# Attention and quantized feed-forward on one core: work moved at both ends of the attention loop

## The chip, the cores and the metric

The kernel runs on one core of one Trainium2 chip. The metric is device microseconds of one launch, lower is better. Times of before are from three runs, and from one profiled execution whose trace is quoted below.

## The reference

The input x is 16 batches of 512 rows of 256 numbers. Per batch, with LN a normalization over the last axis without weights:

```python
x = x + attention(LN(x))
x = x + ffn(LN(x))
# attention: 16 heads of 16 columns; xh is LN(x) cut into heads
xw  = einsum('bhtd,hde->bhte', xh, w_att_val)
att = softmax(einsum('bhte,bhse->bhts', xw, xh) / sqrt(16))
o   = einsum('bhts,bhsd->bhtd', att, (LN(x) @ wv_w.T + wv_b) in heads) @ out_w.T + out_b
# ffn: every operand of every product first goes through fp4_quant_dequant (blocks of 16)
gate, up = fp4_linear(y, w_gate), fp4_linear(y, w_up)      # 704 columns
ffn      = fp4_linear(silu(gate) * up, w_down)
```

fp4_quant_dequant divides each block of 16 by its scale (largest magnitude / 6), rounds to the FP4 grid and multiplies back.

## The kernel before

Three blocks of engine programs follow each other, with a barrier of all engines between them. Rows stay in SBUF in x_all, 64 tiles of 128 rows (four per batch), for the whole kernel. "Tile n" of the feed-forward part is row n of x_all.

**first_block** loads batches 0 and 1, normalizes batch 0, turns it, and casts it into a high and a low part (xh and xl, likewise qh and ql, together the tile splits) for exact products in a fast format. SyncE stores these to DRAM (x_rows, q_rows; semaphores stored0 and stored1, one per half of the heads) and reads them back as stacks: x_stack and q_stack of a quad (four heads) hold 64 rows per head pair, so that one product gives scores exact to float32. load_stacks (L146) issues six DMAs per quad; stack_loaded of a quad counts them. VectorE's low_q (L337) makes ql, statistics (L312) starts the normalization of batch 1, and v_dense, the values, comes last (L364).

**attention_block** works in quads, 64 of them, each in four steps j. For quad i+2 TensorE makes score products of queries by keys into a ring of PSUM banks (max_scores, L769) and VectorE reduces each to row maxima (reduce_max, L1058); GpSimd splits the maxima in two (split_maxima, L595), VectorE turns them, and ScalarE's queue stores them to DRAM and loads them back as max_stack (store_maxima, L988, load_maxima, L994). For quad i TensorE makes the scores of keys by queries and adds the maxima by a second product (key_scores, L782), ScalarE takes exponentials (L924), TensorE weighs the values (weigh_values, L793). In the gaps (IN_STEP) stand the preparation of batch b+1 ("x0", "q0", "x1", "q1", "v0", "v1") and the end of batch b-1: "rows" (turn the weighed values), "turn0" and "turn1" (turn the normalized outputs), "proj0" and "proj1" (output projection, then the residual add on VectorE, L1127). The order of each engine is written out by hand; semaphores alone connect them. SyncE stores and loads stacks of batch b+1 during batch b (L745). ScalarE's queue opens the block with copy_weights (L1012), twelve DRAM to DRAM DMAs into slabs, which batch b quantizes three at a time. After the loop, the rest of batch 15 is finished on its own (rows3, turn0, turn1, proj0, proj1).

Before the first batch stands a prologue of sixteen max_scores calls (two products each), quads 0 and 1; the first step's scores follow it:

```python
for g in range(2):
    for n in range(PAIRS * TT):
        max_scores(-1, g + 2, n)
pe.wait_ge(pool_set, POOL_SET)
batch(0)
```

**ffn_block** works in rounds n, each engine with its own body(n, u). In round n TensorE does turn_h(n-1), gate_up(n+1), turn_x(n+2), down(n-1) (L1433); VectorE normalizes tile n+4, quantizes tile n+3, multiplies gate by up for tile n and quantizes that (L1301). x's absolute values and the gates are ScalarE's, the scaling back GpSimd's. Rounds begin at -5: `ROUNDS = (-5, (1, TILES // 4 - 2), TILES + 2, 4)`, so rounds -5 to 0 fill the pipeline.

## Time and profile before

| What | us |
|---|---|
| median of 3 runs (1507.13 to 1508.17) | 1507.44 |
| profiled execution | 1504.88 |
| its span | 1502.9 |
| busy: TensorE | 1427.5 (95%) |
| busy: VectorE | 1267.9 (84%) |
| busy: ScalarE | 865.6 (58%) |
| busy: GpSimd | 658.7 (44%) |

PE is TensorE's products and PEld its weight loads, DVE is VectorE, ACT is ScalarE, POOL is GpSimd; ACTq and SPq are the DMA issues of ScalarE and SyncE. A timeline row gives start, duration, engine, line, what is written from what, the count, and in brackets how long the engine was idle before and what released it. An x16 of fp32 products is eight calls. The granted clock of TensorE is a share of 2.4 GHz, so 0.50 is 1.2 GHz.

### The profile page before, as it was taken

Reading aid. Unit: us, or ns where it says so; the run is one execution under the profiler, and the core shown is the slowest. Engines: PE = TensorE matmul, PEld = TensorE weight load, DVE = VectorE, ACT = ScalarE, POOL = GpSimd, SP = SyncE. Lnnn points to the kernel's source line nnn. Section 1 sums busy time; section 2 is a strip of 40 time slices with the busy share of each in tenths; the row PEclk is TensorE's granted clock in tenths of the full one; section 3 lists DMA queues with packets and bytes.
Section 4 is the critical chain, followed back from the end, with each engine's and each line's share of the span. In section 5 each row is a group of like instructions: output and inputs, shape, how many; then the busy total and the mean of one; then the engine's idle time right before and its main releaser. Section 6 shows DMA issues by size and latency. Waiting matters only on the chain. (4 is left out here: it accounts for less than half of the span.)

```text
span 1502.9 us, 32223 instructions
## 1 busy us (share of the span) xinstructions
PE 1427.5 (95%) x8562; PEld 886.5 (59%) x8562; DVE 1267.9 (84%) x2644; ACT 865.6 (58%) x1730; POOL 658.7 (44%) x910
## 2 busy tenths in 40 slices
PE   3799999999999999999999998699999999999998
PEld 2355555555555555555555554467777777777776
DVE  4888888888888888888888883499999999999995
ACT  1477777777777767777777767333333333333332
POOL 2346546546546546545545421143434434343341
PEclk7799999999999999999999999899999999999999
DMA  8655555555555556556555460000000000000000
GB/s 235 174 150 163 144 142 167 139 140 169 138 140 173 136 138 175 134 138 176 133 138 168 119 170 16 0 12 18 14 17 14 17 14 17 17 14 17 14 18 22
DMA packets 99433, 148.09 MB, mean 99 GB/s; under 512 B 20928, under 2 KB 58176, under 8 KB 99392
## 3 DMA queue, kind: packets, MB, share of 16 engines
q1 hardware_dynamic: 76832, 135.38, 33.0%
q10 hardware_dynamic: 22560, 12.21, 3.2%
q8 instruction: 21, 0.34, 0.1%
q14 instruction: 20, 0.16, 0.0%
HBM read 85.02 MB, written 65.27 MB: 100 GB/s over the span
## 5 line engine op out<-in xcount | busy, mean ns | idle before, releaser
L1064 DVE TENSOR_REDUCE neg_max<-ring 128x1 f32<-128x512 f32 x1024 | 642.8, 682 | 109.8 <-PE ring L779 106.2
L924 ACT ACTIVATE probs<-scores 128x512 f32<-128x512 f32 x1024 | 531.4, 603 | 189.7 <-PE scores L790 178.0
L1410 PE MATMUL gu_bank<-splits,f_x_T 128*128 128x352 f32 x1024 | 315.4, 462 | 0.9 <-ACT f_x_T L1388 0.9
L779 PE MATMUL ring<-x_stack,q_stack 64*128 64x512 f32 x1024 | 234.3, 456 | 33.5 <-DVE neg_max L1064 18.7
L806 PE MATMUL ring<-probs,v_quad 128*32 128x512 f32 x2048 | 247.3, 601 | 4.2 <-DVE neg_max L1064 4.1
L1410 PEld LDWEIGHTS gu_bank<-splits,f_x_T 128*128 128x128 f32 x1024 | 190.7, 191 | 96.8 <-ACT f_x_T L1388 1.6
L779 PEld LDWEIGHTS ring<-x_stack,q_stack 64*128 64x128 f32 x1024 | 98.5, 188 | 189.4 <-DVE neg_max L1064 138.0
L787 PE MATMUL scores<-q_stack,x_stack 64*128 64x512 f32 x1024 | 206.8, 399 | 2.6 <-ACT probs L924 2.6
L790 PE MATMUL scores<-max_stack,max_ones 64*128 64x512 f32 x1024 | 203.3, 392 | 0.0
L1243 POOL TENSOR_TENSOR f_rstd<-f_mean_var,eps 128x1 f32<-128x1 f32 x64 | 43.2, 676 | 294.5 <-DVE f_mean_var L1354 294.5
L623 POOL TENSOR_TENSOR pv_rows<-pv_more,pv_rows 128x512 f32<-128x512 f32 x64 | 82.0, 1282 | 198.9 <-ACT pv_more L930 198.9
L1373 ACT ACTIVATE h_T<-h_bank 128x512 f32<-128x512 f32 (+1 forms) x128 | 55.8, 488 | 173.1 <-PE h_bank L1420 173.1
L1428 PE MATMUL y_bank<-splits,h_T 128*128 128x256 f32 x640 | 148.9, 380 | 1.1 <-ACT h_T L1373 1.1
L806 PEld LDWEIGHTS ring<-probs,v_quad 128*32 128x32 f32 x2048 | 54.0, 109 | 126.4 <-issue 77.3
L1428 PEld LDWEIGHTS y_bank<-splits,h_T 128*128 128x128 f32 x640 | 116.9, 191 | 14.8 <-DVE x_all L1344 0.8
L787 PEld LDWEIGHTS scores<-q_stack,x_stack 64*128 64x128 f32 x1024 | 97.6, 186 | 24.0 <-ACT probs L924 12.6
L790 PEld LDWEIGHTS scores<-max_stack,max_ones 64*128 64x128 f32 x1024 | 97.4, 186 | 20.7
L1253 POOL TENSOR_TENSOR hq<-h_level,h_scale 128x704 f32<-128x704 f32 x64 | 88.7, 1385 | 30.0 <-DVE h_level L1299 30.0
L600 POOL TENSOR_TENSOR max_cols<-neg_max,one 128x16 fp32r<-128x16 f32 x64 | 13.8, 216 | 183.6 <-DVE neg_max L1064 183.6
L1388 ACT ACTIVATE f_x_T<-x_bank 128x256 f32<-128x256 f32 x64 | 24.6, 384 | 119.5 <-PE x_bank L1398 119.4
L1294 DVE SCALAR_TENSOR_TENSOR h_level<-h_mag,h_units 128x704 f32<-128x704 f32 x64 | 57.1, 892 | 41.5 <-ACT h_mag L1366 41.5
L1380 ACT ACTIVATE gate<-gu_bank 128x352 f32<-128x352 f32 x128 | 58.7, 458 | 41.1 <-PE gu_bank L1410 41.1
(115 smaller groups left out, 1983.6 us busy)
## 6 DMA issues: line engine op xcount, KB each, us to landing
x_rows<-splits SPq DMA_DIRECT2D x128, 256.0 KB, 3.0
x_stack<-x_rows SPq DMA_DIRECT2D x128, 256.0 KB, 4.3
q_stack<-q_rows SPq DMA_DIRECT2D x256, 128.0 KB, 4.3
q_rows<-splits SPq DMA_DIRECT2D x64, 256.0 KB, 2.2
out_dram<-x_all SPq DMA_DIRECT2D x64, 128.0 KB, 1.7
x_all<-in_L_attn_x_dram ACTq DMA_DIRECT2D x14, 512.0 KB, 4.1
w_raw<-slabs SPq DMA_DIRECT2D x14, 192.0 KB, 4.4
slabs_kept<-w_turned SPq DMA_DIRECT2D x14, 192.0 KB, 4.3
```

The source lines that it names most:

```text
L623: pool.tensor_tensor(pv_rows[g % 2][:, :], pv_more[:, :], pv_rows[g % 2][:, :], ALU.add)\
L779: pe.matmul(bank(tiles[m])[:, :], row_tile(q_stack[q], m)[:, p, s * P:(s + 1) * P], row_tile(x_stack[q], m)[:, p, :], start=True, stop=Tru ...
L787: pe.matmul(scores[ROWS * p + m][:, :], row_tile(x_stack[g], m)[:, p, j * P:(j + 1) * P], row_tile(q_stack[g], m)[:, p, :], start=True, st ...
L790: pe.matmul(scores[ROWS * p + m][:, :], row_tile(max_ones, m)[:, 0, :], row_tile(max_stack[g % 2], m)[:, p, :], start=False, stop=True).th ...
L806: m = pe.matmul(bank(tile)[VW * h:VW * h + VW, :], v[q][:, j, h, :], probs[j][:, k, :], start=(j == steps[0]), stop=(j == steps[1]))
L924: act.activation(probs[j][:, k, :], scores[k][:, :], ACT.Exp).then_inc(p_ready, 1)
L1064: dve.tensor_reduce(neg_max[g % 2][:, at:at + 1], tile[:, :], AX.X, ALU.max, negate=True).then_inc(m_used, 1)
L1253: pool.tensor_tensor(blocks(out), blocks(level), spread(scale, BLK), ALU.mult).then_inc(done, 1)
L1294: dve.scalar_tensor_tensor(out=level, in0=mag, scalar=SHIFT_MIN, in1=units, op0=ALU.max, op1=ALU.subtract).then_inc(step, 1)
L1380: act.activation(gate[1 - u][:, k, :], gu_bank[k][:, :], ACT.Silu).then_inc(gate_done, 1)
L1410: m = pe.matmul(gu_bank[c][:, :], x_T[u][:, a, :], gate_up_T[:, a, c * CH:(c + 1) * CH], start=(a == 0), stop=(a == HALVES - 1))
L1428: m = pe.matmul(y_bank[:, :], h_T[u][:, k, :], down_T[k][:, :], start=(k == 0), stop=(k == len(SLICES) - 1))
```

## The change

The change has four parts. *Stores and loads of batch 0:* before the first barrier only the first half of the heads is stored and only quad 0 is loaded, x_stack by SyncE and q_stack by ScalarE; quad 1, the second half's stores and quads 2 and 3 follow the barrier. VectorE's low_q(0) comes before statistics(1). *First scores:* the scores of quad 0's first step stand inside the prologue, before the sixth max_scores call of quad 1 (AHEAD = 5). *Weight copy:* the twelve DMAs move from ScalarE's queue to SyncE's, behind all stack loads of batch 0 and a wait for quad 0's maxima. *Seam:* the class FirstX holds the steps on x of the feed-forward part, on tiles of attention that are free by then (v_dense, raw_x, raw_q); tiles 0 and 1 are quantized and tile 2 normalized in quads 2 and 3 of batch 15, and the rounds begin at -1 (TensorE and ScalarE: -2). The end of batch 15 moves into these rounds. The turned maxima of quad 1 are also taken two reductions sooner.

```diff
@@ first_block, SyncE, ScalarE, VectorE
-            for a in range(HALVES):
-                sp.wait_ge(xl_done, a + 1)
-                store(a, x_rows, (xh, xl, xl, xh))
-            for a in range(HALVES):
-                sp.wait_ge(ql_done, a + 1)
-                store(a, q_rows, (qh, ql))
-
+            sp.wait_ge(xl_done, 1)
+            store_parts(sp, 0, 0, x_rows, (xh, xl, xl, xh), stored)
+            sp.wait_ge(ql_done, 1)
+            store_parts(sp, 0, 0, q_rows, (qh, ql), stored)
             sp.wait_ge(bias_loaded, 32)
-            for g in range(2):
-                load_stacks(sp, 0, g, x_stack, q_stack, x_rows, q_rows, stored, stack_loaded)
+            sp.wait_ge(stored[0], STORES)
+            load_x_stack(sp, 0, 0, x_stack, x_rows, stack_loaded)
...
             move(1)
+            act.wait_ge(stored[0], STORES)
+            load_q_stack(act, 0, 0, q_stack, q_rows, stack_loaded)
...
             low_x(1)
+            low_q(0)
             dve.wait_ge(x_second, 16)
             statistics(1)
-            low_q(0)
             low_q(1)
@@ attention_block, one batch early on VectorE, ScalarE, GpSimd
+    EARLY_DVE = {(2, 0): (("statistics", 0), ("statistics", 1)), (2, 1): (("normal", 0), ("statistics", 2)),
+                 (2, 2): (("units", 0), ("normal", 1), ("statistics", 3)),
+                 (3, 0): (("levels", 0), ("units", 1), ("normal", 2)), (3, 2): (("levels", 1),)}
+    EARLY_ACT = {(2, 3): 0, (3, 1): 1}
+    EARLY_POOL = {(2, 1): (("deviation", 0), ("deviation", 1)), (2, 2): (("deviation", 2),), (2, 3): (("deviation", 3),),
+                  (3, 1): (("back", 0),), (3, 3): (("back", 1),)}
@@ attention_block, SyncE
+            load_x_stack(sp, 0, 1, x_stack, x_rows, stack_loaded)
+            store_parts(sp, 0, 1, x_rows, (xh, xl, xl, xh), stored)
+            store_parts(sp, 0, 1, q_rows, (qh, ql), stored)
             for g in range(2, QUADS):
                 load_stacks(sp, 0, g, x_stack, q_stack, x_rows, q_rows, stored, stack_loaded)
+            sp.wait_ge(max_loaded[0], 16 * ROWS)
+            copy_weights()
             sp.wait_ge(w_copied, 16 * COPIES)
             load_weights(0)
             batch(0)
@@ attention_block, TensorE
             for g in range(2):
                 for n in range(PAIRS * TT):
+                    if (g, n) == (1, AHEAD):
+                        pe.wait_ge(pool_set, POOL_SET)
+                        step_scores(0, 0, 0, True)
                     max_scores(-1, g + 2, n)
-            pe.wait_ge(pool_set, POOL_SET)
...
             weigh_values(B, 0, True)
-            for kind in [kind for kind in ALL if kind in FINISH]:
-                other(kind, B)
@@ attention_block, ScalarE
-            copy_weights()
+            load_q_stack(act, 0, 1, q_stack, q_rows, stack_loaded)
             store_maxima(0, 0)
             load_maxima(0, 0)
...
             end_half(LAST, QUADS - 1)
-            turn("turn0", B)
-            turn("turn1", B)
@@ ffn_block
-    ROUNDS = (-5, (1, TILES // 4 - 2), TILES + 2, 4)
+    EARLY = -1
+    ROUNDS = ((1, TILES // 4 - 2), TILES + 2, 4)
...
+            pool.tensor_tensor(pv_rows[1][:, :], pv_more[:, :], pv_rows[1][:, :], ALU.add).then_inc(end_summed, 1)
...
+                if isinstance(n, int) and n == -1:
+                    weigh_last()
+                if isinstance(n, int) and n == 0:
+                    add_last()
...
+                if isinstance(n, int) and n in (-2, 0):
+                    a = (n + 2) // 2
+                    act.wait_ge(end_turned, a + 1)
+                    act.activation(o_T[a][:, :], turn_bank[a], ACT.Copy).then_inc(end_moved, 1)
...
+                if isinstance(n, int) and n == -2:
+                    turn_last(0)
+                if isinstance(n, int) and n == -1:
+                    rows_last()
+                if isinstance(n, int) and n == 0:
+                    pe.wait_ge(end_weighed, 1)
+                    turn_last(1)
+                    pe.wait_ge(end_moved, 2)
+                    project_last(0)
+                    project_last(1)
+                    pe.wait_ge(end_added, 2)
+                    pe.wait_ge(padded, 1)
```

What moves can be seen on two engines at three places. The lines are those of each kernel's own file. First SyncE's queue in the first block, before (x_rows and q_rows are stores, the stacks loads; the pair of stack rows comes four times):

```order
L209 DMA x_rows<-splits 128x512 x8
L209 DMA q_rows<-splits 128x512 x4
L152 DMA x_stack<-x_rows 64x1024
L156 DMA q_stack<-q_rows 32x1024 x2
L152 DMA x_stack<-x_rows 64x1024
L156 DMA q_stack<-q_rows 32x1024 x2
```

and in the change, where the L228 branch is the barrier:

```order
L184 DMA x_rows<-splits 128x512 x4
L184 DMA q_rows<-splits 128x512 x2
L162 DMA x_stack<-x_rows 64x1024 x2
L228 UNCONDITIONAL_BRANCH
L735 UNCONDITIONAL_BRANCH
L162 DMA x_stack<-x_rows 64x1024 x2
L184 DMA x_rows<-splits 128x512 x4
L184 DMA q_rows<-splits 128x512 x2
L162 DMA x_stack<-x_rows 64x1024 x2
L172 DMA q_stack<-q_rows 32x1024 x4
```

Two quads' loads stood ahead of the barrier, and now only quad 0's x part does; the second half's stores follow it.

Second, TensorE from the first barrier on, before (products into the ring are max_scores, the others key_scores):

```order
L767 UNCONDITIONAL_BRANCH
L779 MATMUL ring<-x_stack,q_stack 128x512 x34
L787 MATMUL scores<-q_stack,x_stack 128x512 x2
L790 MATMUL scores<-max_stack,max_ones 128x512 x2
L787 MATMUL scores<-q_stack,x_stack 128x512 x2
L790 MATMUL scores<-max_stack,max_ones 128x512 x2
L779 MATMUL ring<-x_stack,q_stack 128x512 x4
```

and in the change:

```order
L830 UNCONDITIONAL_BRANCH
L842 MATMUL ring<-x_stack,q_stack 128x512 x26
L850 MATMUL scores<-q_stack,x_stack 128x512 x2
L853 MATMUL scores<-max_stack,max_ones 128x512 x2
L850 MATMUL scores<-q_stack,x_stack 128x512 x2
L853 MATMUL scores<-max_stack,max_ones 128x512 x2
L842 MATMUL ring<-x_stack,q_stack 128x512 x12
L850 MATMUL scores<-q_stack,x_stack 128x512 x2
```

The first step's eight score products move from behind all 32 products of the prologue (two of the 34 are batch 0's) to behind the 26th.

Third, TensorE from the last products of attention (L838, L846, L853 are rows3, the turns and the projections; L1410 gate and up, L1420 the transposes of h), before:

```order
L838 MATMUL ring<-ident,pv_rows 128x128 x4
L806 MATMUL ring<-probs,v_quad 32x512 x8
L838 MATMUL ring<-ident,pv_rows 128x128 x4
L846 MATMUL ring<-ident,o_rows 128x128 x8
L853 MATMUL ring<-out_T,o_T 128x256 x8
L563 UNCONDITIONAL_BRANCH
L1392 UNCONDITIONAL_BRANCH
L1398 MATMUL x_bank<-ident,f_xq 128x128 x2
L1410 MATMUL gu_bank<-splits,f_x_T 128x352 x8
L1398 MATMUL x_bank<-ident,f_xq 128x128 x2
L1410 MATMUL gu_bank<-splits,f_x_T 128x352 x8
L1398 MATMUL x_bank<-ident,f_xq 128x128 x2
```

and in the change, from the barrier on (L1576 turn_last, L1582 rows_last, L1589 project_last, L1552 gate and up, L1562 the transposes of h):

```order
L1540 MATMUL x_bank<-ident,v_dense 128x128 x2
L1576 MATMUL h_bank<-ident,o_rows 128x128 x4
L1552 MATMUL gu_bank<-splits,f_x_T 128x352 x8
L1540 MATMUL x_bank<-ident,v_dense 128x128 x2
L1582 MATMUL y_bank<-ident,pv_rows 128x128 x4
L1552 MATMUL gu_bank<-splits,f_x_T 128x352 x8
L1540 MATMUL x_bank<-ident,v_dense 128x128 x2
L1576 MATMUL h_bank<-ident,o_rows 128x128 x4
L1589 MATMUL y_bank<-out_T,o_T 128x256 x4
L1589 MATMUL h_bank<-out_T,o_T 128x256 x4
L1562 MATMUL h_bank<-ident,hq 128x128 x6
L1552 MATMUL gu_bank<-splits,f_x_T 128x352 x8
```

Rows, turns and projections of the last batch now stand among the transposes and gate products of tiles 0 and 1.

## Rows read from the trace of the kernel before

**Rows 1.** The page: the chain that ended last, by line.

```profile
PE gu_bank L1410 19%; PE y_bank L1428 10%; PE h_bank L1420 3%; PE x_bank L1398 1%; POOL hq L1253 0%; POOL f_xq L1253 0%; POOLq L1236 0%; POOL f_rstd L1246 0%; POOL f_rstd L1243 0%; DVE x_level L1294 0%; DVE x_scale L1273 0%; DVE f_stats L1334 0%; DVE h_level L1294 0%; DVE f_xn L1338 0%; DVE x_units L1286 0%
```

**Rows 2.** Windows: us, busy of PE, PEld, DVE, ACT, POOL; PEclk, DMA share, GB/s.

```profile
20.00:30.00 10.00, 1.22 (x4) 0.50 (x4) 2.07 (x4) 0.00 (x0) 2.26 (x4) 0.57 0.95 235
...
950.00:952.00 2.00, 1.95 (x9) 1.58 (x10) 0.68 (x2) 0.08 (x1) 0.00 (x0) 0.50 0.01 4
...
1000.00:1480.00 480.00, 480.00 (x2106) 357.17 (x2105) 440.70 (x1041) 178.79 (x410) 187.24 (x229) 1.00 0.05 16
```

**Rows 3.** Timeline of the first block: start us, us, engine, line, op.

```profile
13.29 1.40 DVE L315 BATCH_NORM_STATS2 stats<-x_all 128x6 f32<-128x256 f32 x4
...
14.60 0.67 DVE L339 SCALAR_TENSOR_TENSOR splits<-q_half,splits 128x512 fp32r<-128x512 f32 x1
...
16.96 2.70 SPq L209 DMA_DIRECT2D q_rows<-splits  x4
...
19.70 1.32 DVE L364 TENSOR_TENSOR v_dense<-v_tiles,v_bias 128x512 f32<-128x512 f32 x2
...
20.76 0.57 SPq L152 DMA_DIRECT2D x_stack<-x_rows  x1
...
26.17 1.05 SPq L156 DMA_DIRECT2D q_stack<-q_rows  x2
...
28.12 1.22 PE L779 MATMUL ring<-x_stack,q_stack 64*128 64x512 f32 x4 [9.21 <-DMA q_stack<-q_rows]
```

**Rows 4.** Timeline, 41 to 56 us: quad 0's maxima and the first scores.

```profile
41.04 0.21 DVE L1073 STREAM_TRANSPOSE max_turned<-max_cols 128x32 f32<-128x32 f32 x1 [0.70 <-POOL max_cols L603]
...
46.48 1.12 ACTq L991 DMA_DIRECT2D max_rows<-max_turned  x1
...
52.64 0.68 PE L787 MATMUL scores<-q_stack,x_stack 64*128 64x512 f32 x2
...
55.07 1.29 DVE L1064 TENSOR_REDUCE neg_max<-ring 128x1 f32<-128x512 f32 x2 [0.90 <-PE ring L779]
```

**Rows 5.** Timeline: the weight copy's first and last issue, batch 1's stores and stack.

```profile
27.62 0.64 ACTq L1021 DMA_DIRECT2D slabs<-in_L_ffn_w_gate_dram  x1
...
45.11 1.32 ACTq L1039 DMA_DIRECT2D slabs<-in_L_ffn_w_gate_dram  x2
...
68.39 0.82 SPq L711 DMA_DIRECT2D q_rows<-splits  x2
...
80.41 0.50 PE L779 MATMUL ring<-x_stack,q_stack 64*128 64x512 f32 x2 [0.84 <-DMA q_stack<-q_rows]
```

**Rows 6.** Timeline of the seam, 942 to 967 us.

```profile
942.46 0.60 ACT L935 ACTIVATE pv_rows<-ring 128x512 f32<-128x512 f32 x1 [0.74 <-PE ring L806]
...
947.80 0.60 ACT L930 ACTIVATE pv_more<-ring 128x512 f32<-128x512 f32 x1 [2.65 <-PE ring L806]
...
953.79 1.97 PE L853 MATMUL ring<-out_T,o_T 128*128 128x256 f32 x8 [0.78 <-ACT o_T L939]
...
958.57 0.69 DVE L1132 TENSOR_TENSOR x_all<-ring,x_all 128x512 f32<-128x512 f32 x1 [2.08 <-PE ring L853]
...
966.99 6.59 PE L1410 MATMUL gu_bank<-splits,f_x_T 128*128 128x352 f32 x16 [0.47 <-ACT f_x_T L1388]
```

**Rows 7.** Timeline of the feed-forward part's first two rounds.

```profile
973.62 0.53 DVE L1312 TENSOR_TENSOR h<-gu_bank,gate 128x352 f32<-128x352 f32 x1 [0.66 <-PE gu_bank L1410]
...
980.12 0.94 DVE L1312 TENSOR_TENSOR h<-gu_bank,gate 128x352 f32<-128x352 f32 x2
...
982.01 0.87 PE L1420 MATMUL h_bank<-ident,hq 128*128 128x128 f32 x6 [2.52 <-POOL hq L1253]
...
982.72 4.90 PE L1410 MATMUL gu_bank<-splits,f_x_T 128*128 128x352 f32 x16
...
988.09 1.38 POOL L1253 TENSOR_TENSOR hq<-h_level,h_scale 128x704 f32<-128x704 f32 x1
...
990.27 0.82 PE L1420 MATMUL h_bank<-ident,hq 128*128 128x128 f32 x6
```

More of the change, by code:

```diff
@@ L882, in quad @@
                         max_scores(b, g, PAIRS * j)
-                    if j == 0:
-                        pe.wait_ge(max_loaded[g], 16 * ROWS * (b + 1))
-                    for p in range(PAIRS):
-                        key_scores(i, g, j, p, start)
+                    if not (start and j == 0):
+                        step_scores(b, g, j, False)
                     if ahead:
@@ L1187, in sb, with scale_back, ffn_block @@
+def scale_back(pool, n, level, scale, out, step, freed, freed_by, done):
+    pool.wait_ge(step, S * (n + 1))
+    wait(pool, freed, freed_by)
+    pool.tensor_tensor(blocks(out), blocks(level), spread(scale, BLK), ALU.mult).then_inc(done, 1)
+def ffn_block(nc, ctx, x_all, ident, gate_up_T, down_T, out, first_x, out_T, pv_rows, pv_more, o_rows, o_T, recip):
     def sb(name, shape, dt=F32):
@@ L1220, in ffn_block @@
     MOVES = 2
-    S = 6
     SLICES = [min(at, I - P) for at, _ in FK]
```

388 lines of the change are left out of this document (243 added, 145 removed).

## The prediction

> **What bounds the kernel now.** I read the chain of waits first. Its largest terms are TensorE's gate and up products and the down products [rows 1], all of the feed-forward part, because the chain is followed back only to the barrier in front of that part. The windows come next: from 1000 to 1480 us TensorE is busy for all of 480.00 us at the full clock, with VectorE at 440.70 [rows 2]. Nothing in the diff changes what those rounds or the attention loop issue, so whatever is won or lost lies at three places where TensorE is not full: the start, attention's first batch, and the seam between attention and feed-forward. I read these in the timeline.
>
> At the start, SyncE issues both halves' stores and then the stack loads of two quads. Its last issue in the first block ends at 27.22 (26.17 + 1.05); across the barrier, TensorE's first score product starts at 28.12, released by a q_stack load [rows 3]. VectorE then reduces 32 tiles up to about 51.9. The first step's scores wait behind all of them, though quad 0's maxima were turned at 41.04: ScalarE's queue was still issuing the weight copy and stored them only at 46.48 [rows 4, 5].
>
> At the seam, the last attention copy on ScalarE ends at 948.40 (947.80 + 0.60), then follow sum, transposes and two projections one at a time until 959.26; the feed-forward part opens with normalizing and quantizing, and its first gate product starts at 966.99. TensorE turns h of tile 0 at 982.01 and h of tile 1 at 990.27 (one steady round later) [rows 6, 7].
>
> **Start: what the change makes of it.** low_q(0) no longer stands behind four statistics (13.29, 1.40 us), but they cost it nothing before either: it ran at 14.60, as they ended, to 15.27, and I leave it there [rows 3]. What moves is SyncE: four x stores, two q stores, and the wait on stored0. The q stores issue from 15.3 to 16.3 (four took 2.70). Before, half 0's went out from 16.96 to 18.3 and the wait ended at 20.76, 2.4 us on; less is queued now, so I take 2.2 and put the first x_stack load at 18.5 [rows 3]. The six loads of quad 0 go out on two queues, two on SyncE and four on ScalarE. From first issue to release it was 7.36 us with quad 1's loads in the same engines; 1 MB at the 235 GB/s of 20 to 30 us is 4.5 us [rows 2, 3]. I take 5.6 us, between them, so data at 24.1. The other gate is the barrier: VectorE's statistics now delay its v_dense adds, which ended at 21.0 (19.70 + 1.32), by 1.3 to 22.3; plus the 0.9 from 27.22 to 28.12 this is 23.2. Data comes last: the first product at 24.1, **-4.0** (bounds -4.9 by the barrier, -2.3 if the loads still take 7.36).
>
> The Trainium skill, DMA: Bandwidth & Descriptors, section "Issuing engines are not separate DMA queues", says that DMAs issued from SyncE and ScalarE share the same 16 DMA engines and interleave, so a second queue saves only issue time. By that rule the term stays at -4.0, since the gain comes from less data ahead of quad 0; if the second queue doubled the rate, the barrier would decide and it would be -4.9.
>
> Quad 1's loads, the second half's stores and quads 2 and 3 now follow the barrier. Quad 1 is wanted 11 us after the first product (16 reductions), quads 2 and 3 after 24: that cover hides them.
>
> *Early scores.* The maxima are turned at 37.0 and stored at once; from store to the first scores it was 6.2 us (46.48 to 52.64), so 43.2 [rows 4]. TensorE meets the wait after five of quad 1's eight pairs, at about 43.2. The eight matmuls cost 1.8 us at the half clock (0.68 for the first pair, overlapping) [rows 4]. VectorE has about two tiles in hand, so it starves for about **+0.8** (0 to 1.9). In exchange the first step of batch 0 has no scores between its two product pairs, and the 0.90 us that VectorE idled at 55.07 goes: **-0.9**. The clock rise that fell into that step falls into the second, whose twelve products take about half again as long: **+0.9** (0 to 1.9). Together the start gives **-3.2**, bounds -5.8 and +0.6.
>
> *The copy.* Twelve issues that took ScalarE's queue 18.8 us (27.62 to 46.43, with 45.11 + 1.32) [rows 5] move to SyncE behind the maxima of quad 0, so 43.2 to at most 62, likely less, as they shared the engines with stack loads. Behind them stand batch 1's x and q stores and stacks, whose q stores went out at 68.39 and whose stack TensorE waited for at 80.41 already, 0.84 us [rows 5]. Shifted by 3.2 they are due at 65.2. A copy that ends by 60 costs nothing; I count 0 and keep 1.5 for the range.
>
> **Seam.** Tiles 0 and 1 are quantized and tile 2 normalized in the last batch. VectorE has no reductions there in quads 2 and 3, and GpSimd is mostly idle. ScalarE's two added absolute values, under half a microsecond each, stand ahead of waits on TensorE like the 0.74 at 942.46 [rows 6]; I cost them at nothing, at most 0.9 if that cover goes.
>
> So the barrier opens after 948.40, TensorE starts 0.9 later (the 27.22 to 28.12 of the first barrier), two transposes and a copy take 1.1 (six transposes 0.87, a copy 0.60), and the first gate product starts at 950.4. It lasted 6.59 after a pause of TensorE, and 4.90 in the steady state [rows 6, 7]. The window 950 to 952, when TensorE had just resumed, shows the clock at 0.50 [rows 2]; the pause ahead of it is shorter now by a sum on GpSimd, so I take 6.0, ending at 956.4. A transpose pair and a copy lie between the tiles, with the last quad's row transposes inside: 0.9. Tile 1's products run 957.3 to 962.1. Then six transposes (0.95). ScalarE first owes h's absolute value, a gate and tile 2's copy: 0.8 more, chosen. Copy 0.60, both projections back to back 3.6 (1.97 each, overlapping), the second residual add 0.69 [rows 6], and 0.2 of handovers: TensorE turns h of tile 0 at 968.95. The h path itself (982.01 - 973.62 = 8.4, from the second half's product, which now waits for the last rows' weighing until 958.6) would allow 967.0, so the projection is last, and this wait is the price of the new place. **-13.1**.
>
> Behind it VectorE is late: round 1 started at 980.12, 1.9 us ahead of 982.01, and took 9.35 to the end of hq at 989.47 [rows 7]. Now it starts with the turning, at 968.9, hq(1) is ready at 978.2 and TensorE, 8.2 after its turn, would be at 977.1: **+1.1**. After that VectorE gains on TensorE. The seam gives **-12.0**, bounds -14.8 (clock up, 1.3 less for the first product; no idle ScalarE, 1.5) and -3.8 (both tiles' products at the half clock, 2 x 9.5 in place of 6.0 + 4.8).
>
> **Sum:** -3.2 - 12.0 = -15.2. The profiled execution took 1504.88 (span 1502.9, 2.0 around it), hence 1489.7; the median of the runs is 1507.44, 2.6 above it, hence **1492.2** us.
>
> **Rivals.** *Idle start.* The early scores wait for maxima that land after 43.2, VectorE starves, and the late copy makes batch 1's stacks late. For it: 43.2 against 43.2, and the 0.84 us at 80.41. Against: it takes 3.2 us of give-back, with the first product earlier by at least 2.3. Time 1507.4 - 12.0 = 1495.4. Chance 0.2. *Warm seam.* The short pause leaves the clock up, and ScalarE is never behind: -3.2 - 14.8, hence 1489.4. For it: the pause is shorter than the one that ended in the half clock. Chance 0.1. *Cold seam.* The clock stays at half until the projection: -3.2 - 3.8, hence 1500.4. For it: the half clock at 950 [rows 2] and the 6.59 of the first product before [rows 6]; against: 6.59 is much nearer to 4.90 than to twice that. Chance 0.06. *Slower.* The copy holds SyncE. From the last copy's landing to quad 0 of batch 1 in place is some 14 us (2.5 for six store issues, and the 11.2 from the end of the q stores at 69.21 to 80.41) [rows 5], due at 77. Each microsecond that the copy lands after 63 is a microsecond of TensorE; at 78 all 15.2 is gone, and from 81.3 on the kernel is slower by more than can be told, 1510.5. For it: its packets now run beside the batch's own loads, as they ran beside stack loads before. Against: it would have to take 38 us where its issues took 18.8. Chance 0.03.
>
> **How the numbers follow.** The forecast has 0.61; its own range is 1488.5 to 1496. With the warm seam and the idle start the range is 1487.5 to 1498.5, which leaves out the cold seam, the slower case and the tails of the unknown costs. A measurement here tells about 0.2%, 3 us, from no change. The four cases below 1504 hold 0.97; 0.03 of it I give to stalls that add up from several bounds at once. Faster 0.94, same 0.03, slower 0.03.
>
> **What would show it.** In the new profile: first score product at 23.2 to 25.8; four scores groups near 43 and ScalarE's first exponentials near 45; the copy on SyncE's queue ending before 62 and no stack wait above 2 us near 77; the first gate product 2 us after the last copy of pv_more; TensorE's h transposes of tile 0 about 18.5 us after it, released by the second residual add and not by hq; the next one a little over 8.2 us on. Wrong would be a first product later than 26, a second step of more than four microseconds, or rounds of other than 8.2 us.

## The result: 1.4% faster, just outside the range

Four timed runs of the changed kernel have a median of 1486.28 us (1485.41 to 1489.65), four of the kernel before beside them 1507.81 us (1507.13 to 1510.37). The ratio is 0.9864, with a 95% interval of 0.9845 to 0.9884: 20.5 us less (17.5 to 23.4). The forecast was 1492.2 with a range from 1487.5, so the time lies 1.2 us below its low end. The direction was right and the gain was undersized by some 5 to 6 us. The experiments show that the loop, put at nothing, gave some 3 us, and that the terms for the start and the seam were each 4 us off, in opposite directions. One of the many timed runs of the kernel before that stand beside the experiments took 2371.92 us at a granted clock of 0.557; it is left out of every ratio and spread below.

| | before | after |
|---|---|---|
| median of the runs, us | 1507.81 | 1486.28 |
| profiled execution, us | 1504.88 | 1486.98 |
| its span, us | 1502.9 | 1485.1 |
| mean granted clock | 0.983 | 0.987 |

I divide both traces at the same work: the start of ScalarE's copy of pv_more, which comes once in each of attention's 64 quads and ends one. The stretches are the span up to the end of quad 1, from there to quad 59, and so on.

| stretch (profiled execution) | before | after | difference |
|---|---|---|---|
| start to quad 1 | 83.98 | 84.97 | +1.0 |
| quad 1 to 59 | 811.30 | 811.43 | +0.1 |
| quad 59 to 60 | 17.77 | 13.98 | -3.8 |
| quad 60 to 63 (the last) | 34.75 | 34.75 | 0.0 |
| quad 63 to the end | 555.1 | 540.0 | -15.1 |

**The start.** The windows of the changed kernel, to be held against [rows 2]:

```profile
20.00:30.00 10.00, 2.62 (x8) 1.08 (x8) 4.93 (x9) 0.00 (x0) 4.82 (x16) 0.57 1.01 251
946.00:960.00 14.00, 12.93 (x54) 8.69 (x55) 10.95 (x28) 6.55 (x13) 3.76 (x6) 1.00 0.00 0
1000.00:1480.00 480.00, 477.54 (x2099) 355.36 (x2098) 435.18 (x1018) 177.32 (x405) 184.32 (x223) 1.00 0.05 17
```

And its timeline from the first block to batch 0, which answers to [rows 3 to 5]:

```profile
14.64 1.39 DVE L337 BATCH_NORM_STATS2 stats<-x_all 128x6 f32<-128x256 f32 x4
14.76 0.84 SPq L184 DMA_DIRECT2D q_rows<-splits  x2
...
17.91 5.46 ACTq L172 DMA_DIRECT2D q_stack<-q_rows  x8
17.97 4.66 SPq L162 DMA_DIRECT2D x_stack<-x_rows  x4
...
25.21 1.22 PE L842 MATMUL ring<-x_stack,q_stack 64*128 64x512 f32 x4 [6.41 <-DMA q_stack<-q_rows]
...
37.42 1.97 SPq L172 DMA_DIRECT2D q_stack<-q_rows  x4
38.13 0.21 DVE L1111 STREAM_TRANSPOSE max_turned<-max_cols 128x32 f32<-128x32 f32 x1 [0.70 <-POOL max_cols L629]
38.37 1.14 ACTq L1061 DMA_DIRECT2D max_rows<-max_turned  x1
...
44.14 0.54 ACTq L1071 DMA_DIRECT2D max_stack<-max_rows  x2
...
46.20 0.68 SPq L779 DMA_DIRECT2D slabs<-in_L_ffn_w_gate_dram  x1
46.31 0.80 PE L850 MATMUL scores<-q_stack,x_stack 64*128 64x512 f32 x2 [2.59 <-DMA max_stack<-max_rows]
...
48.82 1.29 DVE L1102 TENSOR_REDUCE neg_max<-ring 128x1 f32<-128x512 f32 x2 [3.77 <-PE ring L842]
...
53.03 1.22 PE L842 MATMUL ring<-x_stack,q_stack 64*128 64x512 f32 x4 [2.07 <-DVE neg_max L1102]
54.20 1.30 SPq L797 DMA_DIRECT2D slabs<-in_L_ffn_w_gate_dram  x2
...
59.13 0.40 SPq L762 DMA_DIRECT2D w_raw<-slabs  x1
```

The first score product starts 2.9 us earlier (25.21 for 28.12), but it is still the transfer that releases it: 7.30 us from the first issue at 17.91, as long as before with quad 1's loads beside it. In fact quad 1's loads are beside it again. The x4 and x8 of the two stack rows are both quads' loads: quad 0's six are issued by 19.90, and the barrier opens so early that quad 1's follow at 21.53, 3.6 us behind the first issue (before: 24.05, 3.3 us behind). A narrower window shows them:

```profile
21.53 1.11 SPq L162 DMA_DIRECT2D x_stack<-x_rows  x2
21.54 1.32 ACTq L172 DMA_DIRECT2D q_stack<-q_rows  x3
```

From there the lead is lost. Quad 0's maxima are stored at 38.37, and ScalarE can load them only at 44.14, 5.77 us later, while the stack loads of quads 2 and 3 (SyncE's last issue ends at 39.39) are still in the DMA engines. TensorE stands 2.59 us before the early scores, VectorE then idles 3.77 us, and batch 0 begins at 53.03, against 52.08 before. TensorE's clock also comes up later: in the window from 55 to 70 us it is 0.87 on the mean, against 0.98 before.

**The seam** of the changed kernel, which answers to [rows 6, 7]:

```profile
945.13 0.60 ACT L997 ACTIVATE pv_more<-ring 128x512 f32<-128x512 f32 x1 [2.65 <-PE ring L875]
...
946.04 0.41 PE L1540 MATMUL x_bank<-ident,v_dense 128*128 128x128 f32 x2 [0.98 <-PEq L589]
...
946.92 5.00 PE L1552 MATMUL gu_bank<-splits,f_x_T 128*128 128x352 f32 x16
...
952.62 5.00 PE L1552 MATMUL gu_bank<-splits,f_x_T 128*128 128x352 f32 x16
...
959.23 1.99 PE L1589 MATMUL y_bank<-out_T,o_T 128*128 128x256 f32 x8 [0.95 <-ACT o_T L1530]
961.06 1.89 PE L1589 MATMUL h_bank<-out_T,o_T 128*128 128x256 f32 x8
962.99 0.69 DVE L1500 TENSOR_TENSOR x_all<-h_bank,x_all 128x512 f32<-128x512 f32 x1 [1.03 <-PE h_bank L1589]
...
963.73 0.87 PE L1562 MATMUL h_bank<-ident,hq 128*128 128x128 f32 x6 [0.79 <-DVE x_all L1500]
...
972.41 0.88 PE L1562 MATMUL h_bank<-ident,hq 128*128 128x128 f32 x6 [0.26 <-POOL hq L1359]
```

The order of events is the forecast's: TensorE resumes after 0.98 us of idle, the first gate product comes shortly after the last copy, the residual projection between the products, h of tile 0 turned when the second residual add releases it, h of tile 1 in the next round. From the last copy to that second turning it is 27.28 us (972.41 - 945.13) for 42.47 before. The clock is at its upper level throughout: 14 us of window at 1.00, and 5.00 us for the gate products of tile 0, where the old first one took 6.59.

**What was not in the forecast** is the stretch from quad 59 to 60. Windows of it, kernel before and then changed kernel:

```profile
903.00:913.00 10.00, 7.93 (x40) 3.72 (x40) 4.46 (x8) 6.20 (x12) 0.43 (x2) 0.66 0.05 12
```

```profile
903.00:913.00 10.00, 7.95 (x60) 4.27 (x58) 7.39 (x13) 8.54 (x17) 1.72 (x3) 1.00 0.12 28
```

Before, TensorE's clock fell to half in it for a while (0.66 on average), after it did not. SyncE issues the FFN weight loads just ahead (892.47 to 900.9), and quad 61's maxima, stored at 895.29, were loaded only at 902.56, with ScalarE's exponentials waiting behind that load.

### The profile page after: what moved, and what is told of

It is laid out like the page before. It is cut to its first block and busy times, and to the rows that moved or that the text cites. A ratio compares the mean times of both kernels' runs of the same rounds, so it can differ in the third digit from the quotient of the medians.

```text
span 1485.1 us, 32215 instructions
## 1 busy us (share of the span) xinstructions
PE 1422.1 (96%) x8562; PEld 882.9 (59%) x8562; DVE 1267.9 (85%) x2644; ACT 866.0 (58%) x1730; POOL 659.4 (44%) x910
## 5 line engine op out<-in xcount | busy, mean ns | idle before, releaser
L1552 PE MATMUL gu_bank<-splits,f_x_T 128*128 128x352 f32 x1024 | 313.7, 459 | 0.1
L1552 PEld LDWEIGHTS gu_bank<-splits,f_x_T 128*128 128x128 f32 x1024 | 189.6, 190 | 95.4 <-ACT f_x_T L1526 0.5
L853 PE MATMUL scores<-max_stack,max_ones 64*128 64x512 f32 x1024 | 203.0, 392 | 0.0
L1308 POOL TENSOR_TENSOR f_small<-f_small,eps 128x1 f32<-128x1 f32 x64 | 43.0, 672 | 295.8 <-DVE f_small L1275 295.8
L853 PEld LDWEIGHTS scores<-max_stack,max_ones 64*128 64x128 f32 x1024 | 97.3, 186 | 21.0
L626 POOL TENSOR_TENSOR max_cols<-neg_max,one 128x16 fp32r<-128x16 f32 x64 | 13.9, 218 | 190.2 <-DVE neg_max L1102 190.2
```

Source lines behind the costliest of these rows:

```text
L853: pe.matmul(scores[ROWS * p + m][:, :], row_tile(max_ones, m)[:, 0, :], row_tile(max_stack[g % 2], m)[:, p, :], start=False, stop=True).th ...
L1552: m = pe.matmul(gu_bank[c][:, :], x_T[u][:, a, :], gate_up_T[:, a, c * CH:(c + 1) * CH], start=(a == 0), stop=(a == HALVES - 1))
```

## The experiments

The theories at the outset. **A**: the start is worth nothing in the end; the seam is worth 15 us or more, since the clock stays up in it; the rest is the stall around the FFN weight loads. **B**: the forecast's sum holds, -3 for the start and -12 for the seam, and the rest is chance between executions.

**1. The start alone**, the kernel before with the change's first block, early scores and weight copy on SyncE:

```diff
+                    if (g, n) == (1, AHEAD):
+                        pe.wait_ge(pool_set, POOL_SET)
+                        step_scores(0, 0, 0, True)
...
+            load_x_stack(sp, 0, 1, x_stack, x_rows, stack_loaded)
...
+            sp.wait_ge(max_loaded[0], 16 * ROWS)
+            copy_weights()
```

> The kernel before with the change's start alone (stores, stack loads, first scores, weight copy), the seam as before. Theory A (from the two traces: TensorE stands in front of the early scores until the maxima land, and the first quads end 1 us later than before): 1507 to 1509 us, no gain; the end of quad 59's values about 1 us later than before's 895.3. Theory B (the forecast's sum, start worth -3.2): 1504.6 us, quad 59 at 892. The stretch from quad 59 to quad 60, 17.8 us before and 14.0 in the change, is free to fall either way.

Measured: 1503.05 us median of 12, ratio 0.9973 (0.9959 to 0.9988) to 1507.39, below both theories and nearer to B. But its profile ends quad 1 at 85.94, two microseconds later than before; it gained in the stretch from quad 59 to 60 (14.51). So a part that I had not on the list was at work. Experiment 10 finds it, and that part alone gives the same ratio, 0.9977: nothing is left for the start.

**2. The seam alone**, the change with the start of the kernel before:

```diff
-                    if (g, n) == (1, AHEAD):
-                        pe.wait_ge(pool_set, POOL_SET)
-                        step_scores(0, 0, 0, True)
+            pe.wait_ge(pool_set, POOL_SET)
...
-            sp.wait_ge(max_loaded[0], 16 * ROWS)
-            copy_weights()
```

> The change with its start undone: loads, stores, weight copy and first scores as before, only the seam changed. Theory A (seam worth about 15, since the clock stays up at the first gate product): 1492 to 1493 us, and 25.5 to 27.5 us from the last pv_more copy to the transposes of h of tile 1. Theory B (the forecast, clock down at the first gate product, -12.0): 1495.8 us and 30 us on that stretch.

Measured: 1488.92 of 5, ratio 0.9880 (0.9857 to 0.9904), again below both theories. The last stretch is 539.98 us, that of the change to 0.02. This version also keeps the change's load helpers, and its stretch from quad 59 to 60 is 14.38: the seam and that stretch together carry nearly all of the gain.

**3 and 4. The FFN weight loads held back**, in the change and in the kernel before:

```diff
             sp.wait_ge(w_loaded, 16 * UNITS)
+            sp.wait_ge(max_loaded[3], 16 * ROWS * B)
```

> The change, with the loads of the feed-forward weights (8 DMAs, 2.1 MB, issued at 893.6) held back on SyncE until the maxima of the last quad are in place (about 926). Theory A (they delay the store of quad 61's maxima, for which ScalarE's queue stands with two exponentials undone): the 1.8 us wait of ScalarE and TensorE's idle time at 900 to 906 go, 1483.5 to 1485.5 us. Theory B (that wait is covered elsewhere): 1486.3, no difference. A loss would mean that the weights come too late for the first gate product.

> The same one wait in the kernel before. Theory A: the 2.85 us wait of ScalarE and the 6 us at the half clock behind it go, 17.8 us from quad 59 to 60 become 13.8 to 14, and the kernel takes 1503.5 to 1505 us. Theory B (a stall of one profiled execution that is no part of the median): 1507.8.

Measured: 1487.10 (ratio 0.9869, 0.9844 to 0.9893) and 1504.95 (0.9994, 0.9977 to 1.0011). The profiles have 13.11 and 13.10 us from quad 59 to 60: without the loads in front, the stall is gone. In the times it did not show beyond their spread: 1504.95 lies in theory A's range, but neither ratio differs clearly from that of the same kernel without the hold. Two versions at the end of experiment 9 have the same hold and 13.11 and 13.10 us again.

**5. Without the early scores**: batch 0's first scores at its head again, all else as in the change (the first four lines of the diff of 2).

> The change with one part undone: batch 0's first scores are issued at the head of batch 0 again, behind all sixteen reduced tiles, not between the fifth and sixth pair of quad 1. Theory A (the early scores wait for maxima that land late, and cost more than they return): TensorE's wait of 2.6 us for the maxima and VectorE's idle of 3.8 us go, the first step gets back its 0.9 us gap, and the end of quad 0 comes 0.5 to 2 us earlier than in the change; the median 0.5 to 2 us below the change's 1486.3 (ratio to the kernel before 0.985 to 0.986). Theory B (the early scores return more than they cost): the end of quad 0 comes 0.5 to 2 us later and the median is 1487 to 1489.

Measured: 1483.97 of 6, ratio 0.9846 (0.9822 to 0.9871), on theory A's side, though the interval still overlaps that of the change's 0.9864. Quad 0 ends at 69.65 for 70.89. Quad 1 ends at 83.24 and, in a second execution, at 83.26, 2.4 us before the mean of seven executions with the change's start (85.6) and 1.3 before that of seven with the old one (84.6). In the profiles the early scores cost more than the rest of the start brings.

**6. Quads 2 and 3 loaded late**:

```diff
+            sp.wait_ge(max_loaded[0], 16 * ROWS)
             for g in range(2, QUADS):
                 load_stacks(sp, 0, g, x_stack, q_stack, x_rows, q_rows, stored, stack_loaded)
-            sp.wait_ge(max_loaded[0], 16 * ROWS)
             copy_weights()
```

> The change, with SyncE issuing the stack loads of quads 2 and 3 only once quad 0's maxima are loaded, and the weight copy behind them. Theory A (those loads, issued at 33 to 39 us, are what makes the maxima, stored at 38.4, land at 44.1 and not at 41.7): the maxima land at 41 to 42.5, TensorE's wait for them is under 0.5 us, VectorE's idle of 3.8 us falls under 2, and the end of quad 0 comes 1.5 to 3 us earlier than the change's 70.89, unless quad 2's stack is late. Theory B (the time from store to landing is the transfers' own): the maxima land no earlier than 43.5, nothing is gained, and quad 2's stack, wanted at 53, lands late and costs 0 to 3 us.

ScalarE's queue and TensorE in its timeline:

```profile
38.28 1.14 ACTq L1061 DMA_DIRECT2D max_rows<-max_turned  x1
40.37 0.54 ACTq L1071 DMA_DIRECT2D max_stack<-max_rows  x2
...
43.44 0.63 PE L850 MATMUL scores<-q_stack,x_stack 64*128 64x512 f32 x2
...
50.02 1.22 PE L842 MATMUL ring<-x_stack,q_stack 64*128 64x512 f32 x4 [2.07 <-DMA q_stack<-q_rows]
```

From store to load it is now 2.09 us in place of 5.77, the early scores start at 43.44 with no wait, and quad 1 ends at 82.02 (81.40 in a second execution). That is what delayed the early scores: the maxima's way to DRAM and back stood behind quad 2's and 3's stacks. The timed runs do not follow fully: 1486.91 of 6, ratio 0.9868 (0.9844 to 0.9892), level with the change, though both profiled executions took 1482.3 and 1484.5.

**7. A pause in the seam**: TensorE waits, before it turns tile 0's x, until GpSimd has made the last sum and four fillings that nothing uses.

```diff
+                    if isinstance(n, int) and n == -2:
+                        pe.wait_ge(end_summed, 1)
                     turn_x(n + 2, u)
```

> The change, with TensorE made to wait before it turns tile 0's x for the feed-forward part until GpSimd has made the last quad's sum and four fillings of 128x704 that nothing uses: some 5 to 6 us of pause in place of 1.0. Theory A (the length of the pause sets the clock of the first products): the granted clock falls to half after it, tile 0's gate products take 6.5 to 9.6 us in place of 5.00, and the turning of h of tile 0 comes 7 to 10 us later than in the change. Theory B (the pause alone is lost, the clock stays up): the gate products take 4.9 to 5.1 us and the turning of h of tile 0 comes later by the pause's own 4 to 5 us, less what the residual projection hid.

```profile
951.11 0.69 PE L1546 MATMUL x_bank<-ident,v_dense 128*128 128x128 f32 x2 [5.52 <-POOL hq L1435]
951.59 1.06 PE L1582 MATMUL h_bank<-ident,o_rows 128*128 128x128 f32 x4
952.45 5.87 PE L1558 MATMUL gu_bank<-splits,f_x_T 128*128 128x352 f32 x16
...
959.01 5.00 PE L1558 MATMUL gu_bank<-splits,f_x_T 128*128 128x352 f32 x16
```

```profile
950.00:955.00 5.00, 3.89 (x12) 2.91 (x13) 0.00 (x0) 2.46 (x4) 1.00 (x2) 0.66 0.00 0
```

Measured: 1494.74 of 5, ratio 0.9919 (0.9893 to 0.9946). After 5.52 us of pause (0.98 in the change) the clock is at half at first (theory A's mechanism, at less than its price): 0.66 over that window, two transposes in 0.69 for 0.41, and the gate products in 5.87 for 5.00. Both h of tile 0 and h of tile 1 are turned 5.86 us later (33.14 for 27.28 from the last copy for tile 1), where A had 7 to 10: 4.5 is longer pause, and the other 1.3 is clock. My 6.0 for that product, with a pause said to be shorter only by GpSimd's sum, was the right price for a pause more than five times as long as the one that came.

**8. Without the projection in the seam.** It leaves out turning the second half of batch 15's o, its output projection and its residual add, so those rows hold x alone.

```diff
-                    turn_last(1)
-                    pe.wait_ge(end_moved, 2)
-                    project_last(0)
-                    project_last(1)
-                    pe.wait_ge(end_added, 2)
+                    pe.wait_ge(end_moved, 1)
```

> The change without turning the first half of the last batch's second half of o, its output projection and its residual add: this leaves out the attention of batch 15 (its whole output projection), whose rows then hold only x. Theory A (the forecast's: the projection holds back the turning of h of tile 0 by 1.9 us against what the h path allows, and part of it is won back later because VectorE is the later one): tile 0's h is turned 1.5 to 4 us earlier after the last copy of pv_more than the change's 27.3 us, and the whole stretch from that copy to the end is 0.5 to 2.5 us shorter than 540.0. Theory B (the projection is hidden behind VectorE's h path): the turning comes at 27.3 and the stretch stays within 0.3 us of 540.0.

```profile
962.63 1.51 PE L1560 MATMUL h_bank<-ident,hq 128*128 128x128 f32 x6 [4.32 <-POOL hq L1359]
963.93 6.85 PE L1550 MATMUL gu_bank<-splits,f_x_T 128*128 128x352 f32 x16
```

Neither theory. h of tile 0 is turned 1.57 us earlier (17.03 us after the last copy for 18.60), near the forecast's 1.9, but TensorE has idled 4.32 us by then and is at half clock: the transposes take 1.51 for 0.87, the next gate products 6.85 for 4.90, and h of tile 1 is turned at 27.83, 0.55 us later than with the projection. Its time is 1487.33 (ratio 0.9870, 0.9836 to 0.9904). The last stretch is 540.50 us for 539.97. So in this place the last projection costs nothing that shows: it fills the wait, and in the executions that had it the clock stayed up.

**9. More executions.** The kernel before was profiled twice more, and the versions of 5 and 6 once more:

> The kernel before, looked at again. Theory A (the stretch from the last copy of pv_more to the end is long and of a different length in each execution, because TensorE pauses in it and its clock comes back at another moment each time): the stretch is not the 555.1 us of the profiled execution but anywhere from 553 to 559, and the stretch from quad 59 to quad 60 (17.8 us) differs too. Theory B (it is set by the program alone): 555.1 and 17.8 within 0.3 us.

> The kernel before, looked at once more: as for the first look. With the two profiles of kernels that keep its seam (554.06 and 557.5 us) and this one there are five, from which the mean gain of the new seam against 540.0 can be taken; theory A expects 16 to 18 us, theory B 15.1.

> The change without the early scores, looked at again, since its profiled execution was its slowest. Theory A (the median tells: without early scores the kernel is some 2 us faster than the change): quad 0 ends before 70.9, the seam is 540.0 us, the time is 1483 to 1485. Theory B (the early scores are worth nothing either way): quad 0 ends at 70 to 72 and the time is 1486 to 1487.

> The change with quads 2 and 3 loaded late, looked at again, since its profiled execution was its fastest. Theory A (the order of the loads is what brings the maxima early): they land at 43.4 or before again, and quad 0 ends at 67 to 69; what makes its other runs 5 us longer than the profiled one then lies behind quad 0. Theory B (the first look was lucky): the maxima land after 44 and quad 0 ends at 70 to 72.

The seam in the first new execution of the kernel before:

```profile
954.14 3.75 PE L853 MATMUL ring<-out_T,o_T 128*128 128x256 f32 x8 [0.78 <-ACT o_T L939]
958.68 3.78 PE L853 MATMUL ring<-out_T,o_T 128*128 128x256 f32 x8 [0.78 <-DVE x_all L1132]
969.78 0.66 PE L1398 MATMUL x_bank<-ident,f_xq 128*128 128x128 f32 x2 [7.32 <-POOL f_xq L1253]
970.91 7.66 PE L1410 MATMUL gu_bank<-splits,f_x_T 128*128 128x352 f32 x16 [0.47 <-ACT f_x_T L1388]
...
987.00 1.54 PE L1420 MATMUL h_bank<-ident,hq 128*128 128x128 f32 x6 [2.52 <-POOL hq L1253]
988.33 5.71 PE L1410 MATMUL gu_bank<-splits,f_x_T 128*128 128x352 f32 x16
```

Both projections ran at half clock here (3.75 and 3.78 us; 1.97 for the same in [rows 6]), the first gate products took 7.66 for 6.59, the next turning and products are slow again, and it lasts 48.03 us from the last copy to the turning of h of tile 1. In six executions with the old seam that stretch was 42.47, 48.03, 41.86, 41.44, 44.90 and 41.65, mean 43.4; in twelve with the new one it was 27.26 to 27.28 each time. So the seam gains 16.1 us on the mean, and the profile I worked from lay 0.9 below the old mean. (In three of the twelve the very last down products ran slower, 4.08 us for 2.40, which lengthens the last stretch to 541.7; that lies outside the seam.) The start also has two faces: the old one ended quad 0 at 69.3 to 70.3 five times and at 73.1 and 73.3 twice; in the three profiled executions of the kernel before, the granted clock of the window from 55 to 70 us was 0.98 where it ended early, and 0.67 and 0.66 where it ended late. The change's start goes the same way: of its seven executions the two that ended quad 0 at 70.2 and 70.9 had 0.86 and 0.87 in that window, the five at 72.0 to 73.4 had 0.65 to 0.72. So part of what this start loses is a clock that comes up late.

Then the change itself, the seam alone, and two mended versions ran on one chip in the same rounds. The first is 5 with the hold of 3, the second 6 with it:

> The change itself, to stand beside the next three on the same chip. Theory A (its start is worth nothing, the early scores take back what the earlier first product gives): 1485.5 to 1487.5 and within 1.5 us of the seam alone. Theory B (the start is worth the forecast's 3.2 us): 2.5 to 4 us below the seam alone.

> The seam alone, with the start of the kernel before. Theory A: within 1.5 us of the change in the same rounds. Theory B: 2.5 to 4 us above it. Its quad 0 ends at 69.5 or at 73.2, the two values that the old start has shown.

> The change without the early scores, and with SyncE's loads of the FFN weights held until the maxima of the last batch's quad 3 are loaded. Theory A (the early scores cost 2 us, the weight loads 0.9 us): quad 0 ends at 69.6, quad 59 to 60 takes 13.1, and the median is 2 to 3.5 us below the change in the same rounds, 1483 to 1484.5. Theory B (neither counts in timed executions): within 1 us of the change.

> The change with quads 2 and 3 loaded after quad 0's maxima, and the same hold of the FFN weight loads. Theory A (what the profile shows holds in timed executions): quad 0 ends at 67.9, quad 59 to 60 takes 13.1, and the median is 4 to 5 us below the change in the same rounds, 1481.5 to 1482.5. Theory B (the profiled executions of this start are not like the timed ones, in which it gained nothing): 0 to 1.5 us below the change, and above the version without early scores.

| version | median, us | ratio to before (1506.97), 95% |
|---|---|---|
| the change | 1487.33 | 0.9861 (0.9832 to 0.9890) |
| the seam alone | 1487.05 | 0.9861 (0.9835 to 0.9887) |
| no early scores, weights held | 1483.58 | 0.9839 (0.9814 to 0.9865) |
| quads 2, 3 late, weights held | 1483.39 | 0.9835 (0.9810 to 0.9859) |

The change's start is worth nothing in timed runs either. The mended versions lie 3.8 and 3.9 us below the change in the same rounds, near the ends of what their theories A had, the second with its slowest run (1484.27) below the change's fastest (1485.27). They have the lowest medians of all that ran, and beat both kernels; which of the two is better can't be told, nor how much of the gain is the start and how much the hold. The second did not end quad 0 at 67.9 as expected but at 70.26, and quad 1 at 84.17. Up to batch 0 its profile is that of 6 (first product at 49.96, for 49.95 in 6's second execution), and then the clock comes up later. The window from 55 to 70 us, in 6's second execution and in this version:

```profile
55.00:70.00 15.00, 13.02 (x95) 6.53 (x91) 11.96 (x22) 11.50 (x24) 9.65 (x14) 0.98 0.86 264
```

```profile
55.00:70.00 15.00, 14.12 (x82) 6.56 (x80) 10.27 (x19) 9.92 (x20) 8.15 (x12) 0.75 0.67 204
```

A start with 3 us of lead at batch 0 can thus lose most of it by the end of quad 1. This may be why 6's timed runs gained nothing; no timed run has a trace that would show it.

**10 and 11. The order of a quad's stack loads.** All kernels with a part of the change and without the hold of 3 had 13.7 to 14.7 us from quad 59 to 60 (11 executions), the kernel before 17.77, 16.18 and 17.63. What they share is that load_stacks was split in two helpers, and so issues x, x, q, q, q, q where it had x, q, q, x, q, q; SyncE's two listings ahead of the prediction show it. I put that order alone into the kernel before, and the old one back into the change:

```diff
         sp.dma_start(row_tile(x_stack[g], m)...)
+    for m in range(ROWS):
+        h = h0 + PAIRS * m
         src = q_rows[bass.ds(b, 1), a, :, :, h:h + PAIRS, :]
```

> The kernel before, with the order of a quad's six stack loads alone taken from the change (both x loads, then the four q loads). Theory A (the order is what shortens the last batch's stall): quad 59 to 60 takes 13.7 to 14.7 us at the full clock, and the median is 2 to 4 us below the kernel before. Theory B (the order counts for nothing): 16 to 18 us with the clock down, and a median within 1.5 us of the kernel before.

> The change, with the old order of the six loads (x, q, q, x, q, q) in the helper that loads all stacks but those of quads 0 and 1 of the first batch. Theory A: quad 59 to 60 takes 16 to 18 us with the clock down, and the median is 2 to 4 us above the change's 1486.3 to 1487.3. Theory B: 13.7 to 14.7 us and 1486 to 1487.5.

The load of quad 61's maxima in the first and in the second:

```profile
896.64 0.56 ACTq L993 DMA_DIRECT2D max_rows<-max_turned  x1
902.91 0.54 ACTq L1003 DMA_DIRECT2D max_stack<-max_rows  x2
903.50 1.08 ACT L926 ACTIVATE probs<-scores 128x512 f32<-128x512 f32 x2 [1.85 <-DMA max_rows<-max_turned]
```

```profile
897.52 0.56 ACTq L1069 DMA_DIRECT2D max_rows<-max_turned  x1
904.46 0.54 ACTq L1079 DMA_DIRECT2D max_stack<-max_rows  x2
905.04 1.09 ACT L999 ACTIVATE probs<-scores 128x512 f32<-128x512 f32 x2 [2.51 <-PE scores L861]
```

```profile
903.00:913.00 10.00, 7.89 (x48) 3.97 (x44) 5.37 (x9) 6.20 (x12) 0.44 (x2) 0.73 0.28 73
```

Theory A in both directions. With the new order the kernel before takes 1502.65 (12 runs; ratio 0.9977, 0.9961 to 0.9994) and 14.05 us for the stretch; with the old order the change takes 1490.66 (ratio 0.9893, 0.9867 to 0.9920) and 17.55. The second time is 3.3 to 4.4 us above the change's, which did not run in the same rounds, and the intervals of the ratios touch; the stretch is the firmer sign. From store to load of the maxima it is 6.27 us in the one and 6.94 in the other, ScalarE's idle 1.85 for 2.51. That is 0.7 us of the 3.5; the rest goes with the clock, 0.73 in the window above and 1.00 in the same window of the other. The longer wait does not bring the clock down by itself, though: the second execution of the seam alone, with the new order, had 6.98 us from store to load and TensorE waiting 1.36 us, and its clock stayed up (14.73 us for the stretch), while here TensorE waited 1.33 us and it fell:

```profile
904.38 0.50 PE L815 MATMUL scores<-q_stack,x_stack 64*128 64x512 f32 x2 [1.36 <-ACT probs L953]
```

```profile
906.18 0.50 PE L858 MATMUL scores<-q_stack,x_stack 64*128 64x512 f32 x2 [1.33 <-ACT probs L999]
```

So the order is shown as the cause of the shorter stretch, and how it acts on the clock is open. Why x loads first shorten the maxima's way was not tried either.

## Why the prediction missed

Start, middle and seam were forecast as -3.2, 0 and -12.0. The means over all profiled executions are +1.0 (old and new start in seven each, to the end of quad 1; they spread over 82.9 to 86.9), -3.3 (three executions of the kernel before, two of the change) and -16.1. The sum is -18.4. The ratio of the timed runs says -20.5 and the difference of their medians -21.5, and the interval, -17.5 to -23.4, holds all three. Start and seam together come to -15.1 for the forecast's -15.2. That is luck: the two terms were 4.2 and 4.1 us off and cancelled, and without the loop the time would have fallen within the range.

- **"Nothing in the diff changes what those rounds or the attention loop issue" was false for the loop**, and it is the step that cost the range. The set of loads is the same, their order is not, and the helper is called once per quad. I read the diff for what it adds and removes there, not for the order in which two loops in a row issue what one loop had issued. The term is -3.3 on the mean of the profiled executions; putting the order in or taking it out moved the stretch by 3 to 4 us (17.2 to 14.05, 13.9 to 17.55) and the medians by 3.3 to 4.4.
- **Start, first product**: -4.0 forecast, -2.9 measured in the profiled pair. Of the two ends for the loads I took 5.6, worked out from a rate, over 7.36 from a row; the row was right (7.30). The whole gain is the earlier first issue (17.91 for 20.76). The premise that less data stands beside quad 0 was false: I had the barrier held by VectorE's v_dense until 22.3, it ended at 21.25 (19.97 + 1.28), and quad 1's loads went out at 21.53. By the Trainium skill, DMA: Bandwidth & Descriptors, section "Issuing engines are not separate DMA queues", a second issuing queue saves only issue time. The trace agrees that it moves no data faster: quad 0's six issues took 1.99 us on two queues for 3.25 on one, and the release came 7.30 us after the first for 7.36.
- **Start, early scores**: +0.8 forecast as VectorE's idle, 3.77 measured. From the maxima's store to the scores it took 7.94 us (38.37 to 46.31) for the forecast's 6.2, and 5.16 in experiment 6. The 6.2 was taken from a place where the ScalarE queue's copies, not stack loads, were beside it, and I added nothing for the stacks of quads 2 and 3 issued just ahead. One of the signs of being wrong came as well: the second step took 4.31 us (55.86 to 60.17), over the four named, with the clock at half for most of it. The rival *Idle start* named this wait, with what lands late, and gave the sum 1495.4; its wait for the maxima came true (the late stacks did not: batch 1's cost TensorE 0.55 us for 0.84 before), and its place in the sum was overrun by the other two terms.
- **The copy**: 0 forecast, right. SyncE had it issued from 46.20 to 55.50 and went on to batch 1's w_raw at 59.13.
- **Seam**: every event came in the order forecast. In the profiled pair it gave -15.2 for -12.0. From the last copy's start, the first gate product came at 1.8 us for 2.6 (-0.8), took 5.00 for 6.0 (-1.0, the clock stayed up, as *Warm seam* had it), the projection started at 14.1 for 16.6 (-0.7 more, ScalarE was never behind), and the second turning followed the first by 8.68 for 9.3 (-0.6).
- **Base**: the sum was made against one execution, and the spread of the kernel before (1501 to 1514 us over its timed runs) was taken as a shift of 2.6. But part of what varies is the old seam's and the old quad 59's own cost, and a change that removes them gains the mean of it. The profiled pair shows -15.2 for the seam, the mean is -16.1.

## What to carry to other kernels

The tensor engine's pauses of 4.3 to 7.3 us cost their length here plus what the clock took back, and the second part differed from one execution to the next: a change that closes such a pause gains the mean over executions, so profile several before sizing it, and expect the spread to shrink too (the change's eight runs lie within 5 us, the many more of the kernel before within 14). When a small transfer stands on the path, such as the maxima here, ask what large transfers were issued just ahead of it; moving those behind it brought the maxima 3.7 us sooner here, more than the 2.9 by which the whole started sooner, though what of it lasts depends on when the clock comes up. And a refactoring of a DMA helper is a change of its order: compare the sequence on the queue, not the set.

## What the hardware showed that I had not expected

- Filling a wait of TensorE with the projection made the kernel no slower than leaving that work out: without it TensorE idled 4.32 us, and 1.57 us of lead turned into 0.55 us of loss at half clock (one execution).
- After a pause of 0.98 us the granted clock stayed at its upper level (2.4 GHz, 1.00 in the rows); after pauses of 4.32, 5.52 and 7.32 us the products that followed ran at the lower one (1.2 GHz, 0.50 in the rows) for a while, and for how long differed between executions: behind the same 7.32 us the sixteen gate products took 6.35 to 7.66 us in six executions with the old seam, and 6.59, 6.90 and 7.66 in the three of the kernel before. Shorter waits went both ways: after 1.36 us the clock stayed up in one execution, after 1.33 us it fell in another.
- The store of 16 columns of maxima and the wait for their reload took 2.09 us between issues with quiet DMA engines (busy share 0.05 in experiment 6, 38.3 to 40.4 us) and 5.77 behind the twelve stack loads of quads 2 and 3 (0.88 in the change, 38.3 to 44.2 us).
- Timed runs and profiled executions can stand apart by more than either spreads: without early scores 1486.7 and 1486.9 profiled against 1482.1 to 1484.3, with quads 2 and 3 late 1482.3 and 1484.5 against 1485.5 to 1487.7. Why was not found; a clock that comes up late, as in the windows of experiment 9, could do it; that is not shown. For effects of 2 us at the start I go by the timed runs.
